# GpSimd takes weight splits, the first output projection runs on split parts, and a PSUM bank per output tile

## The reference, cut to what matters

```python
x  = L0_attn_x                                     # (2, 512, 256): 2 sequences of 512 tokens, 256 features
xn = layernorm(x)
# recurrent branch
y    = gelu(xn @ w_y + b_y)
xb   = xn @ w_x + b_x
conv = conv_b + sum_k conv_w[k] * shift(xb, 3 - k) # 4 taps along the tokens
gate_x = sigmoid(conv @ w_ig + b_ig)
gate_a = sigmoid(conv @ w_ag + b_ag)
a    = exp(-8 * gate_a * softplus(a_param))
mult = sqrt(1 - a * a)                             # first token: a = 0, mult = 1
h    = scan(h = a * h + gate_x * conv * mult)      # over 512 tokens
attn = (h * y) @ w_out + b_out
# feed-forward branch, weights made ternary: s = mean|w|, q = clip(round(w / s), -1, 1) * s
ffn  = (silu(xn @ w1q.T) * (xn @ w3q.T)) @ w2q.T   # hidden width 682
out  = x + attn + ffn
```

## Time and profile before

| | |
|---|---|
| median of 3 runs | 75.69 us (75.24 to 76.03) |
| profiled execution, its own time | 75.99 us |
| its span in the trace | 74.2 us |
| granted TensorE clock | 1.0 of full speed, all 40 slices |
| busy: PE, VectorE, ScalarE, GpSimd | 69.2, 61.2, 48.3, 31.5 us |
| chain that ended last | PE 80%, DMA 7%, VectorE 5%, SP's queue 3%, issue 1% |

### The profile page before, as it was taken

One profiled execution on the slowest core, in us unless ns is written; L12 is line 12 of the kernel. 1 busy time (PEld: TensorE's weight loads), 2 busy tenths in 40 slices (PEclk: granted clock), 3 DMA queues, 4 the chain that ended last, 5 costly groups with the idle time before them and its releaser, 6 DMA issues.

```text
span 74.2 us, 1064 instructions
## 1 busy us (share of the span) xinstructions
PE 69.2 (93%) x364; PEld 58.6 (79%) x364; DVE 61.2 (82%) x101; ACT 48.3 (65%) x75; POOL 31.5 (43%) x43
## 2 busy tenths in 40 slices
PE   4999969999999999999999999999999999999920
PEld 4985758877888888888888888888899999988800
DVE  4897499999999999999979974697960799999750
ACT  3674523899999999999998978466699910000000
POOL 6385647245851680016002979947689000000000
PEclk9999999999999999999999999999999999999999
DMA  0889999920000000000000000000000000000195
GB/s 8 236 289 333 368 379 342 379 97 9 0 0 0 4 0 0 0 0 0 4 1 0 0 9 0 0 0 0 0 0 0 0 0 0 9 0 0 61 322 183
DMA packets 5095, 5.63 MB, mean 76 GB/s; under 512 B 525, under 2 KB 4578, under 8 KB 5090
## 3 DMA queue, kind: packets, MB, share of 16 engines
q1 hardware_dynamic: 4946, 5.55, 22.1%
q10 hardware_dynamic: 144, 0.01, 0.1%
HBM read 4.51 MB, written 1.05 MB: 75 GB/s over the span
## 4 chain that ended last, share of the span: by engine, by line
PE 80%; DMA 7%; DVE 5%; SPq 3%; issue 1%; DVEq 0%
PE slot L664 25%; PE slot L647 23%; PE slot L696 14%; PE slot L706 8%; DMA x_sb<-x 7%; PE slot L767 4%; PE slot L673 2%; SPq L186 2%; DVE stats L436 2%; PE slot L740 2%; DVE x_sb L551 1%; PE slot L636 1%; DVE xt_lo L455 1%; SPq L183 1%; DVEq L52 0%
## 5 line engine op out<-in xcount | busy, mean ns | idle before, releaser
L256 POOL TENSOR_TENSOR g_lo<-w_raw,g_hi 128x512 fp32r<-128x512 f32 x10 | 14.1, 1421 | 9.0 <-ACT g_hi L338 8.9
L664 PE MATMUL slot<-xt_hi,w_q 128*128 128x512 f32 x40 | 15.7, 393 | 0.0
L664 PE MATMUL slot<-xt_lo,w_q 128*128 128x512 f32 x40 | 15.7, 393 | 0.0
L514 DVE SCALAR_TENSOR_TENSOR w_raw<-w_raw,s,slot 128x512 f32<-128x512 f32 x10 | 7.3, 747 | 3.1 <-ACT w_raw L332 3.0
L696 PE MATMUL slot<-w_q,g_hi 128*128 128x256 f32 x40 | 9.7, 283 | 0.0
L696 PE MATMUL slot<-w_q,g_lo 128*128 128x256 f32 x40 | 9.7, 283 | 0.0
L492 DVE SCALAR_TENSOR_TENSOR conv<-slot,par,conv 128x511 f32<-128x511 f32 (+2 forms) x12 | 9.0, 748 | 0.4
L664 PEld LDWEIGHTS slot<-xt_hi,w_q 128*128 128x128 f32 x40 | 7.5, 188 | 1.7
L664 PEld LDWEIGHTS slot<-xt_lo,w_q 128*128 128x128 f32 x40 | 7.5, 188 | 1.7
L332 ACT ACTIVATE w_raw<-slot,scale 128x512 f32<-128x512 f32 x10 | 6.6, 684 | 3.1 <-PE slot L664 3.1
L696 PEld LDWEIGHTS slot<-w_q,g_lo 128*128 128x128 f32 x40 | 7.7, 192 | 0.0
(11 more groups left out here) (111 smaller groups left out, 144.5 us busy)
## 6 DMA issues: line engine op xcount, KB each, us to landing
w_raw<-w13t SPq DMA_DIRECT2D x2, 682.0 KB, 7.6
w_raw<-dense SPq DMA_DIRECT2D x5, 256.0 KB, 5.6
out<-x_sb SPq DMA_DIRECT2D x3, 256.0 KB, 2.2
w_raw<-w2t SPq DMA_DIRECT2D x1, 640.0 KB
x_sb<-x SPq DMA_DIRECT2D x4, 128.0 KB, 2.3
x_sb<-x SPq DMA_DIRECT2D x1, 512.0 KB, 5.3
out<-x_sb SPq DMA_DIRECT2D x2, 128.0 KB, 2.1
w_raw<-w2t SPq DMA_DIRECT2D x2, 42.0 KB
```

The costliest lines, as they stand in the source:

```text
L256: nc.gpsimd.tensor_tensor(g_lo[:, j, s], g[:, n % RING], g_hi[:, j, s].bitcast(f32), ALU.subtract).then_inc(g_lo_set, 1)
L514: nc.vector.scalar_tensor_tensor(out=g[:, n % RING], in0=silu[:, n % RING], scalar=s32[:, 0:1], in1=slot[H_SLOT[s][j]][:, 1], op0=ALU.mult ...
L664: mm = nc.tensor.matmul(slot[H_SLOT[s][j]][:, o], w13_q[:, c, col:col + P], v[:, s, c], start=(c == 0 and v is xt_hi), stop=(c == KC - 1 a ...
```

## The change

- GpSimd now does: the addition of EPS to the variance, the three small operations of the decay rate (`rates`), the rounded parts of WIG, WAG and of the bias (`square_hi`, `tensor_copy`), both parts of WOUT (behind `squares(1)`), and the rounded part of the last g. Its `w_lo` of WY is cut into two chunks, with the two halves of the second sequence's `rstd` between them.
- The second sequence of x is loaded in two halves and normalised in two halves. VectorE does `xt_lo_of(0)` ahead of the second sequence's statistics. The corrections of the first three tokens (`heads`) are one operation for a sequence.
- VectorE's `tail_hi` stands ahead of `g_of(4)` and `tail_lo` behind it. ScalarE's square roots stand directly behind `silu_of(9)`; ScalarE then rounds h·y of sequence 0 (`hy_hi`), and VectorE subtracts (`low_output`, twice). `project_split(0)` runs on these parts: 24 fp32r matmuls in the place of 8 fp32 ones (16 instructions).
- Sequence 1's four output tiles have a bank each, so there are six additions and six stores; two of the stores are issued by ScalarE.
- On PE, the two small warm-up groups go, one is placed between the transposes, and the first projections take their terms in another order.

```diff
-            sp.dma_start(x_sb[:, 1], x_dram[1]).then_inc(x_loaded[TILES], 16)
+            for i in range(2):
+                t = slice(i * TILES // 2, (i + 1) * TILES // 2)
+                sp.dma_start(x_sb[:, 1, t], x_dram[1][:, t]).then_inc(x_loaded[TILES + i], 16)
...
+            def square_hi(m):
+                pool.wait_ge(w_loaded[m], 16)
+                nc.gpsimd.tensor_copy(w_hi[:, m], w_raw[:, m]).then_inc(w_hi_set, 1)
...
+            square_lo(WY, range(0, 1))
+            rstd_of(1, slice(0, TILES // 2), 3)
+            rstd_of(1, slice(TILES // 2, TILES), 4)
+            pool.wait_ge(xn_set, 2 * TILES)
+            square_lo(WY, range(1, KC))
+            rates()
+            for m in (WIG, WAG):
+                square_hi(m)
+                square_lo(m)
             for s in range(SEQS):
                 for c in range(KC):
                     lo_of_conv(s, c)
+            pool.wait_ge(b_out_loaded, 16)
+            nc.gpsimd.tensor_copy(b_split[:, 0], b_row[:, :]).then_inc(b_hi_set, 1)
             pool.wait_ge(b_hi_set, 1)
             nc.gpsimd.tensor_tensor(b_split[:, 1], b_row[:, :], b_split[:, 0].bitcast(f32), ALU.subtract).then_inc(b_split_set, 1)
-            for n in range(2 * FULL):
+            pool.wait_ge(a2_set, SEQS)
+            square_hi(WOUT)
+            square_lo(WOUT)
+            last = 2 * FULL - 1
+            for n in range(last):
                 lo_of_g(n)
+            pool.wait_ge(g_set, last + 1)
+            nc.gpsimd.tensor_copy(g_hi[:, HJ[last][1], HJ[last][0]], g[:, last % RING]).then_inc(g_hi_set, 1)
+            lo_of_g(last)
...
-            g_hi_of(2 * FULL - 1)
+            g_hi_of(2 * FULL - 2)
+            silu_of(2 * FULL - 1)
             for s in range(SEQS):
                 for c in range(KC):
                     mult_of(s, c)
+            for c in range(KC):
+                act.wait_ge(hy_set, c + 1)
+                act.wait_ge(ga_psum, 1)
+                nc.scalar.activation(hy_hi[:, c], tx[:, 0, c], ACT.Copy).then_inc(hy_hi_set, 1)
+            store(act, 3)
+            store(act, 5)
...
+            def low_output(c):
+
+                dve.wait_ge(hy_hi_set, c + 1)
+                nc.vector.tensor_tensor(hy_lo[:, c], tx[:, 0, c], hy_hi[:, c].bitcast(f32), ALU.subtract).then_inc(hy_lo_set, 1)
...
                     scan(s, c)
+                    if 0 < KC * s + c <= KC:
+                        low_output(KC * s + c - 1)
                     gated_output(s, c)
...
+            dense_terms(slot[Y_SLOT[0]], WY, [(w_hi, xt_hi[:, 0]), (w_hi, xt_lo[:, 0])], True, False)
+            transposes(1, first_half)
+            pe.wait_ge(w_lo_set, KC * WY + 1)
+            dense_terms(slot[Y_SLOT[0]], WY, [(w_lo, xt_hi[:, 0])], False, True, chunks=[0])
+            transposes(1, second_half)
+            pe.wait_ge(w_lo_set, KC * WY + 2)
+            dense_terms(slot[Y_SLOT[0]], WY, [(w_lo, xt_hi[:, 0])], False, True, chunks=[1]).then_inc(y_psum, 1)
...
-            for s in range(SEQS):
-                project(s)
+            project_split(0)
+            project(1)
```

More of the change, by code:

```diff
@@ L375, in _ @@
             newest_tap(0)
-            square_hi(WIG)
             xt_hi_of(1)
@@ L416, in _ @@
             g_hi_of(4)
-            for n in range(FULL, 2 * FULL):
+            for n in range(FULL, 2 * FULL - 1):
                 silu_of(n)
@@ L441, in variance @@
                     nc.vector.bn_aggr(mv[:, s, t], stats[:, s, t]).then_inc(mv_set, 1)
-                dve.wait_ge(mv_set, TILES * s + tiles.stop)
-                t = slice(tiles.start, tiles.stop)
-                nc.vector.tensor_scalar(v_eps[:, s, t], mv[:, s, t, 1], EPS, None, ALU.add).then_inc(v_set, 1)
             def normalise(s, tiles, ready):
@@ L611, in _ @@
             g_of(3)
+            tail_hi()
             g_of(4)
-            g_of(5)
-            tail_hi()
-            g_of(6)
-            g_of(7)
             tail_lo()
-            g_of(8)
-            g_of(9)
+            for n in range(FULL, 2 * FULL):
+                g_of(n)
             for s in range(SEQS):
@@ L630, in _, with transposes @@
         def _(pe):
-            def transposes(s):
-                for t in range(TILES):
+            def transposes(s, tiles):
+                for t in tiles:
                     pe.wait_ge(xn_set, TILES * s + t + 1)
@@ L639, in transposes, with dense_terms @@
                         mm.then_inc(xt_psum, 1)
-            def dense_terms(dst, m, terms, first, last, chunk_ready=None):
-                for c in range(KC):
+            def dense_terms(dst, m, terms, first, last, chunk_ready=None, chunks=range(KC)):
+                for c in chunks:
                     if chunk_ready:
@@ L697, in down, with project_split @@
                                                  stop=False, skip_group_check=True)
+            def project_split(s):
+                pe.wait_ge(w_lo_set, KC * (WOUT + 1))
+                for c in range(KC):
+                    for k, (v, w, ready) in enumerate(((hy_hi, w_hi, hy_hi_set), (hy_hi, w_lo, hy_hi_set), (hy_lo, w_hi, hy_lo_set))):
+                        pe.wait_ge(ready, c + 1)
+                        for i, tiles in enumerate(O_TILES[s]):
+                            for t in tiles:
+                                mm = nc.tensor.matmul(out_tile(s, i, t), v[:, c, t * P:(t + 1) * P], w[:, WOUT, c],
+                                                      start=False, stop=(c == KC - 1 and k == 2), skip_group_check=True)
+                            if c == KC - 1 and k == 2:
+                                mm.then_inc(o_psum, 1)
             def project(s):
@@ L709, in project, with warm @@
                             mm.then_inc(o_psum, 1)
[L711 removed]
+            def warm(count, cols):
                 for _ in range(count):
[L713 removed]
+                    nc.tensor.matmul(slot[WARM_SLOT][:, 0, 0:cols], ones[:, :], ones[:, 0:cols], start=True, stop=True)
+            first_half, second_half = range(0, TILES // 2), range(TILES // 2, TILES)
             pe.wait_ge(ones_set, 1)
[L716 to L720 removed]
+            warm(WARM, P)
             pe.wait_ge(ident_set, 1)
[L722 removed]
+            transposes(0, first_half)
+            warm(1, P // 2)
+            transposes(0, second_half)
             def sums_of_w13():
@@ L755, in _ @@
-            transposes(1)
-            dense_terms(slot[Y_SLOT[0]], WY, [(w_hi, xt_lo[:, 0])], False, True).then_inc(y_psum, 1)
+            for h in range(2):
+                first_x_terms((w_hi,), xt_hi, xt_hi_set, h)
+            first_x_terms((w_hi,), xt_lo, xt_lo_set, 0)
+            pe.wait_ge(w_lo_set, KC * (WX + 1))
+            for h in range(2):
+                first_x_terms((w_lo,), xt_hi, xt_hi_set, h)
+            first_x_terms((w_hi,), xt_lo, xt_lo_set, 1).then_inc(xb_psum, 1)
+            pe.wait_ge(w_hi_set, WY + 1)
```

126 lines of the change are left out of this document (60 added, 66 removed).

## The result

The changed kernel takes 76.94 us (median of 4 runs, 76.53 to 77.38). The kernel before took 75.72 us beside it (75.24 to 76.03). The ratio is 1.017, with a 95% interval of 1.011 to 1.024, so the change made the kernel slower by more than 1%, and the time lies above the predicted range (74.6 to 76.5).

The account below looks back on a forecast made before the run. The prediction took PE as the bound, VectorE nearly as full. Outputs at 68.50 - 0.9 + 1.1 = 68.7 ended the span at 74.1 (-0.1): own time 75.9, less 0.3 for the median, 75.6 us; range 74.6 to 76.5.

Parts of the forecast that it names:

- Gates: From the second sequence's first projection to hidden(0): PE needs 17.5 us, taps end at 25.0, GpSimd's parts free beside them.
- the prediction's own rule: Two-operand VectorE work from SBUF and GpSimd work exclude each other, the later waiting out the first; PSUM-operand work is free.
- The ternary weights: Behind the taps: ready at 31.9, with the bias's copy (0.4) and split (0.7) ahead of ternary_13; squares end at 38.1.
- Hidden blocks and roots: Behind the squares: PE's slot for hidden(8) +0.4, silu(9) ends at 53.85, first root at 55.85 for 57.72, -1.9.
- Last g: Before VectorE's last chain: g_lo(9) holds the first product to 57.0, so the roots' -1.9 shrinks to -0.9.
- Low outputs: VectorE's last chain: two more operations at 0.55 us each, +1.1; outputs start at 68.7.
- Start: Loads and normalising: PE begins the second sequence's first projection at 14.7 instead of 15.71, -1.0.
- The unknown price: GpSimd's rounding copy of 128x512, which had no row: taken as 0.70 us, range 0.52 to 1.29.
- GpSimd becomes the bound: Rival: a copy of 1.29 us delays GpSimd's queue and the last chain, giving 76.6 us; chance 0.19.
- The end: Last additions and stores: the 0.39 wait for PE's last bank falls away, -0.3; span ends at 74.1, -0.1.
- The first rival: VectorE's last chain: first product not held by g_lo(9), outputs start at 67.8, time 74.7 us; chance 0.27.

Follow-up runs that it names:

- The first experiment: Changed kernel with heads(0) moved ahead of the second xt_lo: 76.45 us, ratio 1.012 against the kernel before.
- the ninth kernel: Changed kernel with heads(0) ahead of the second xt_lo, bias operations between the two sequences' low parts, last g's parts on VectorE, split kept: 74.98 us, ratio 0.994.
- experiment 11: Changed kernel with heads(0) ahead of the second xt_lo and last g's parts on VectorE, bias operations left in place, split kept: 75.57 us, ratio 1.003.
- Experiments 2: Changed kernel with GpSimd's two bias operations moved ahead of the four low parts of the convolution: 76.90 us.
- experiment 4: Changed kernel without project_split, both low outputs and WOUT's parts; first sequence projected in f32 as before: 75.96 us, ratio 1.002.
- experiment 10: Changed kernel, heads(0) early, bias between the sequences' low parts, last g on VectorE, only the first projection chunk of sequence 0 split: 74.51 us, ratio 0.988.
- experiment 7: Kernel before with roots directly behind silu(9), g_hi(8) ahead of it and last g's parts on VectorE: 76.18 us, ratio 1.003.
- the eighth kernel: Changed kernel with heads(0) early, last g's parts on VectorE, projection unsplit, bias operations between the two sequences' low parts: 74.88 us, ratio 0.993.
- experiment 6: Old tail order (tail_hi behind g(5), tail_lo behind g(7)): in the changed kernel 77.65 us; in one with four further edits 77.81 us.

## Why the prediction was wrong

**The step that failed is "Gates".** It put the taps' start "behind the second xt_lo at 15.4" and their end at 25.0, and GpSimd's copies and w_lo of WIG and WAG "beside them, free". PE was to start hidden(0) at 32.2 and started it at 33.47. The taps themselves are indeed free of GpSimd: six take 4.54 us with a w_lo beside them and without. But `heads(0)` stands in the row ahead of them with both operands in SBUF, and the step has no term for it: it stood at nothing. By the prediction's own rule it had to wait for the whole of the w_lo. It did (1.06 us), and what follows the taps starts 0.84 us later than before (25.71 for 24.87). The first experiment removes the hold, and the outputs come 1.16 us sooner. Without the holds the rest of the step is right: in the ninth kernel PE needs 17.45 us from the second sequence's first projection to hidden(0) (14.94 to 32.39), for 17.5 predicted.

**The ternary weights** were put at 31.9; they were ready near 32.7. The bias operations were expected ahead of `ternary_13`, 1.1 us in all. They stand behind the last low part of the convolution, which ended at 28.19, and so they fell beside w_q from 28.84 on: both stretched each other, 0.63 us on VectorE. That is the place in the queue and not the late taps: in experiments 1 and 11, with the taps on time, w_q takes 3.85 as well. Squares ended at 39.34 for the predicted 38.1. Experiments 2 and 11 show this term, and experiment 11 shows how it came through: by the longer hold of `gated_input(1)`.

**Hidden blocks and roots.** With VectorE late, hidden(9) and silu(9) were late: silu(9) ended at 55.66 for the predicted 53.85. The gap between silu(9) and the table load fell away as forecast (54.99, 55.67, 56.97 directly behind each other). Of this 1.8, the late squares are 1.2. The other 0.6 is the step's own: from the end of the squares to the end of silu(9) it had 15.75 us, and it is 16.3 here and in the ninth kernel. That the ninth kernel's silu(9) ended at 53.97, close to 53.85, is partly luck, since its squares ended 0.5 sooner than predicted (37.63). The holds in this step were sized well: the second cast of `tail_hi` took 1.67 us for 0.69 [the row at 46.05], 0.98 for the 1.1 predicted, though it has one operand, which the prediction's rule did not name; `tail_lo` took 1.43, where 1.07 passed behind the g_lo before, about 0.4 as predicted. The undisturbed rows were summed too short: from `gated_input(1)` to g(5) it is 8.2 us (42.54 to 50.75) for 7.8. That `gated_input(1)` would be held by WOUT's w_lo was forecast as 0.65 and is 0.75 (1.97 for 1.22).

**Last g.** The product was forecast as held, near 1.8 us long. It was, 1.43 long, at a cost of 0.74. The rival that it is not held is refuted.

**Low outputs** were put at 0.55 each. A chunk with one takes 3.05 us and one without 2.66, so each costs 0.39; this term was too dear, by 0.3 in all.

**Start.** PE was to begin the second sequence's first projection at 14.7 and did at 14.92. The gain of 0.8 was real. At hidden(0) PE was 0.42 behind the kernel before (33.47 for 33.05): 0.55 of the loss is the wait for the taps at 21.20. In the ninth kernel, which starts this projection at 14.94, there is no such wait.

**The unknown price.** GpSimd's copy took 0.61 us, for 0.70 taken, inside the bounds 0.52 to 1.29. The Trainium skill, GPSIMD Engine Reference, section Performance versus the Vector engine, has 1.03 cycles an element, from which the prediction made an estimate of about 0.6. This row bears it out. So the rival "GpSimd becomes the bound" named the right sign for a wrong reason: it needed a dear copy, and slower came with a cheap one.

**The end** was to gain 0.3 from the missing wait. It did not: from the first output to the end of the span are 5.6 us after and 5.7 before. So the wait of 0.39 cost nothing there, nor did 0.45 (experiment 4, 5.6) or 0.51 (experiment 10, 5.7); with 0.53 in experiment 7 the stretch is 5.9, and with 1.22 in the eighth kernel 6.4. A likely reason, not shown, is that the stores of the first outputs still fill the DMA while VectorE waits.

Together, on the first output: 68.7 predicted, +1.8 for the late silu(9), +0.1 from its end to the product (2.16 us for 2.05), less 0.4 for the smaller hold (0.74 for 1.1) and less 0.3 for the low outputs, is 69.9, and 69.98 was measured. Of the 1.8, 1.2 is the lateness of the squares, which lies wholly in "Gates". The first rival's outputs at 67.8 are 67.6 by the prediction's own terms; nothing hangs on it, since the product was held.

A difference between two spans is not one between two medians: the first experiment's span is 1.2 us shorter than that of after, its median 0.5. The profiled execution of after lay 0.44 above its median, that of experiment 1 lay 0.24 below; that is the 0.7 between them. The front alone moved by 0.5 to 0.6 us between executions (experiments 6 and 11), and why it does stays open. The removed warm-ups, the new order of the terms, the second sequence in halves and the banks of the outputs were not tried one by one.

## What to carry to other kernels

Where two engines share a lock, list every instruction that takes it and not only the long ones: a six-element operation took 1.06 us for 0.15, and 2.84 with GpSimd's queue packed. Move such an operation ahead, or place the other engine's work in a gap that already waits, and after each move look again at what now abuts. A gain at one engine's end (the roots, the split) is worth something only when what feeds it is on time: the same change was 1.7% slower with its holds and 0.6% faster once three of them were gone, against the kernel before; with half the split it was 1.2% faster.

## What the hardware showed that was not expected

A VectorE instruction that waits for the lock is passed over by GpSimd instructions that follow one another closely: 2.29 us behind one running subtraction and the next, 2.84 behind one and the two behind it. It got in where the next GpSimd instruction came 0.28 us later (experiment 11: 0.57 us), and in the changed kernel at 16.57, though a GpSimd copy's row starts at 16.49. Whether a copy always lets it in was not tried. Nor is it only work with two operands that is held: casts with one operand in SBUF took 1.67 us for 0.69 and 0.59 for 0.43 behind a running g_lo. And the cost of such a hold is not stable: in experiment 6 `heads(0)` came 0.03 us ahead of the w_lo and was not held, in the changed kernel 0.26 behind its start and took 1.06.
